# Full attention in a one-core Trainium2 kernel: the turn of a head's result, moved to the shift and undivided

## What is computed

```
h = rmsnorm(X, norm1_w)
q = (h @ wq).reshape(B, S, N_HEADS, D_HEAD)      # k, v likewise
scores = jnp.einsum('bshd,bthd->bhst', q, k) * scale
attn = jax.nn.softmax(scores, axis=-1)
ctx = jnp.einsum('bhst,bthd->bshd', attn, v).reshape(B, S, d)
X = X + ctx @ wo
```

## Time and profile before

| | |
|---|---|
| median of 3 runs | 2958.49 us (2955.47 to 2960.29) |
| the profiled execution | 2950.91 us |
| its span, first to last instruction | 2949.1 us |
| busy: TensorE, VectorE, ScalarE, GpSimd | 88%, 74%, 52%, 10% of the span |
| the full attentions' heads | from 1095 to 1784 us and from 2055 to 2744 us |

### The profile page before, as it was taken

How to read it: one execution, slowest core, us unless ns; L and a number is a source line. 1 busy time by engine, 2 the same in 40 slices (tenths; PEclk the granted TensorE clock), 3 DMA queues, 4 the chain that set the end, 5 groups by cost and what they waited for, 6 DMA issues and landing times. The chain is left out here.

```text
span 2949.1 us, 48804 instructions
## 1 busy us (share of the span) xinstructions
PE 2586.2 (88%) x18006; PEld 1283.9 (44%) x18006; DVE 2196.8 (74%) x5368; ACT 1521.9 (52%) x1907; POOL 291.6 (10%) x598
## 2 busy tenths in 40 slices
PE   6699848789994869999999997995999999999799
PEld 3588725478882531222222215882122222221588
DVE  7644569444445859999999965556999999996554
ACT  2222225432222533777777784222377777778422
POOL 5100021110000110000000001012000000000100
PEclk8799959889996977999999998996799999999899
DMA  2000052000005212111101100001211110110000
GB/s 56 23 16 22 8 124 52 2 23 16 22 8 129 48 42 78 23 23 23 23 15 20 23 2 17 22 11 38 83 23 23 23 23 12 23 23 2 17 22 25
DMA packets 57917, 88.95 MB, mean 30 GB/s; under 512 B 14362, under 2 KB 41184, under 8 KB 57712
## 3 DMA queue, kind: packets, MB, share of 16 engines
q1 hardware_dynamic: 56176, 85.61, 12.4%
q0 software_dynamic: 1536, 0.63, 0.1%
HBM read 57.93 MB, written 26.22 MB: 29 GB/s over the span
## 5 line engine op out<-in xcount | busy, mean ns | idle before, releaser
L1147 DVE TENSOR_REDUCE pair_mx<-ps 128x1 f32<-128x512 f32 x2048 | 1271.1, 685 | 20.1 <-PE ps L990 15.9
L1119 ACT ACTIVATE prob<-ps 128x1024 f32<-128x1024 f32 x1024 | 990.1, 1021 | 249.0 <-PE ps L1025 247.3
L990 PE MATMUL ps<-k_stack,q_stack 48*128 48x512 bf16 x2048 | 642.8, 404 | 55.1 <-PEq L804 12.8
L1039 PE MATMUL ps<-prob,v_head 128*32 128x512 f32 x4096 | 547.2, 606 | 1.3 <-ACT prob L1119 1.0
L990 PEld LDWEIGHTS ps<-k_stack,q_stack 48*128 48x128 bf16 x2048 | 148.6, 93 | 902.4 <-DVE pair_mx L1147 842.7
L1837 DVE TENSOR_TENSOR hid<-silu,ps 128x512 f32<-128x512 f32 x360 | 246.1, 686 | 369.2 <-PE ps L1774 250.3
L1806 ACT ACTIVATE silu<-ps 128x512 f32<-128x512 f32 x360 | 214.7, 597 | 574.6 <-PE ps L1774 566.5
L1025 PE MATMUL ps<-q_stack,k_stack 51*128 51x512 bf16 x2048 | 438.1, 382 | 8.5 <-ACT prob L1119 5.3
L1786 PEld LDWEIGHTS ps<-wd,hid 128*128 128x128 f32 (+1 forms) x2880 | 364.3, 191 | 27.3 <-issue 2.6
L1786 PE MATMUL ps<-wd,hid 128*128 128x128 f32 (+1 forms) x2880 | 368.8, 275 | 0.4
L1774 PE MATMUL ps<-ht_part,wg_part 128*128 128x512 f32 (+1 forms) x1080 | 335.6, 419 | 16.8 <-PEq L311 14.8
(11 more groups left out here) (186 smaller groups left out, 1699.5 us busy)
## 6 DMA issues: line engine op xcount, KB each, us to landing
k_stack<-image_dram SPq DMA_DIRECT2D x96, 192.0 KB, 4.5
q_stack<-image_dram SPq DMA_DIRECT2D x88, 192.0 KB, 4.5
image_dram<-parts SPq DMA_DIRECT2D x4, 1440.0 KB, 12.1
image_dram<-parts SPq DMA_DIRECT2D x4, 1344.0 KB, 9.9
image_dram<-parts SPq DMA_DIRECT2D x4, 960.0 KB, 13.8
image_dram<-parts SPq DMA_DIRECT2D x4, 896.0 KB, 10.9
wg<-in_L_ffn_Wg_dram SPq DMA_DIRECT2D x18, 176.0 KB, 2.3
wu<-in_L_ffn_Wu_dram SPq DMA_DIRECT2D x18, 176.0 KB, 2.4
```

The costliest lines, as they stand in the source:

```text
L990: nc.tensor.matmul(max_bank(n), rows_of(c.q_stack, b, g, ROWS, slice(t * P, (t + 1) * P)), rows_of(c.k_stack, b, g, ROWS, slice(k * CHUNK, ...
L1039: ins = nc.tensor.matmul(out, c.v_head[:, e % 2, kb, :], unit, start=(kb == 0), stop=(kb == TILES - 1), skip_group_check=True)
L1119: nc.scalar.activation(c.prob[:, u % P_UNITS, :], c.ps[:, 2 * (u % 2) * CHUNK:2 * (u % 2) * CHUNK + UNIT], ACT.Exp, scale=scale).then_inc( ...
L1147: nc.vector.reduce_max(mx[:, w:w + 1], max_bank(n), AX.X).then_inc(max_taken.sem, 1)
```

## The change

The turn of head e-1's result now stands in TensorE's order right behind the shift's matmul, ahead of unit 28 of head e (the last head's, as before, at the end of the stage). It goes to bank 3, which is free there as bank 2 is for the shift, and the ring of maxima holds score tiles alone. ScalarE copies the turned result with its sums, undivided, to a new buffer `turned` of 16 x 16 x 9 values a partition, behind its copy of the shift's rows and ahead of exponential 28. Unit 29, whose scores go to banks 2 and 3, waits for that copy too. VectorE's reciprocal and product leave the heads' stage. `output_stage`, for a full attention, begins with four pieces on VectorE, each a reciprocal of 64 sums and a product of 512 values a partition, into `mixed`, which now lies in the second half of `qk`; each piece's transposes wait for it. The windowed attentions are as before.

```diff
@@ full_heads_stage
-    TURN_AT = 24
+    SHIFT_BANK, TURN_BANK = 2, 3
-    place = {}  ... (turns and tiles share the ring's places)
+    place = {(h, w): h * SCORES + w for h in range(HEADS) for w in range(SCORES)}
     def turn(pe, e):
-        n = place["turn", e]
-        pe.wait_ge(*max_taken.after(n - len(MAX_BANKS) + 1))
         pe.wait_ge(*out_taken.after(e + 1))
         for j in range(TPC):
-            ins = nc.tensor.transpose(max_bank(n)[:, j * P:(j + 1) * P], c.out_head[:, e % 2, j * P:(j + 1) * P], c.ident[:])
-        ins.then_inc(max_ready.sem, 1)
+            ins = nc.tensor.transpose(bank(c, TURN_BANK)[:, j * P:(j + 1) * P], c.out_head[:, e % 2, j * P:(j + 1) * P], c.ident[:])
+        ins.then_inc(turned.sem, 1)
     def exp_unit(pe, e, u):
         if u == SHIFT_UNIT and e < HEADS - 1:
             shift_rows(pe, e + 1)
+        if u == SHIFT_UNIT and e:
+            pe.wait_ge(*exp_done.after(unit))
+            turn(pe, e - 1)
         if u == SHIFT_UNIT + 1 and e < HEADS - 1:
             pe.wait_ge(*rows_taken.after(e + 2))
+        if u == SHIFT_UNIT + 1 and e:
+            pe.wait_ge(*turned_taken.after(e))
@@ ScalarE
+            def take_turned(e):
+                act.wait_ge(*turned.after(e + 1))
+                cols = bank(c, TURN_BANK).rearrange("p (j k r) -> p j k r", j=TPC, k=CHUNKS)
+                out = c.turned[:, :, e, :].rearrange("p (k j) r -> p j k r", k=CHUNKS)
+                nc.scalar.activation(out, cols[:, :, :, 0:HD + 1], ACT.Copy).then_inc(turned_taken.sem, 1)
                     if u == SHIFT_UNIT and e < HEADS - 1:
                         take_rows(e + 1)
+                    if u == SHIFT_UNIT and e:
+                        take_turned(e - 1)
             take_out(HEADS - 1)
+            take_turned(HEADS - 1)
@@ VectorE
-            def take_turned(dve, e):
...
-                nc.vector.reciprocal(c.inverse[:], cols[:, :, :, HD]).then_inc(inverted.sem, 1)
...
-                nc.vector.tensor_tensor(out, cols[:, :, :, 0:HD], inverse, ALU.mult).then_inc(max_taken.sem, 1)
@@ output_stage(c, w, dst, divide=False)
             for k in range(CHUNKS):
+                if divide:
+                    pe.wait_ge(*divided.after(k + 1))
                 for t in range(k * TPC, (k + 1) * TPC):
...
+            def divide_piece(k):
+                tiles = slice(k * TPC, (k + 1) * TPC)
+                inverse = c.inverse[:, tiles, :]
+                nc.vector.reciprocal(inverse, c.turned[:, tiles, :, HD]).then_inc(inverted.sem, 1)
+                dve.wait_ge(*inverted.after(k + 1))
+                nc.vector.tensor_tensor(c.mixed[:, tiles, :].rearrange("p t (h d) -> p t h d", d=HD), c.turned[:, tiles, :, 0:HD],
+                                        inverse.rearrange("p t (h o) -> p t h o", o=1).broadcast_to((P, TPC, HEADS, HD)), ALU.mult)\
+                    .then_inc(divided.sem, 1)
+            if divide:
+                for k in range(CHUNKS):
+                    divide_piece(k)
```

More of the change, by code:

```diff
@@ L933, in full_heads_stage @@
     out_taken = c.count("full_out_taken")
-    inverted = c.count("full_sums_inverted")
+    turned = c.count("full_out_turned")
+    turned_taken = c.count("full_turned_taken")
     scale = float(HD) ** -0.5
@@ L1006, in shift_rows @@
             pe.wait_ge(*exp_done.after((e - 1) * EXP_UNITS + SHIFT_UNIT))
-        nc.tensor.matmul(bank(c, 2)[0:PARTS * TILES, 0:P], shift, c.ident16[:], start=True, stop=True).then_inc(rows_ready.sem, 1)
+        nc.tensor.matmul(bank(c, SHIFT_BANK)[0:PARTS * TILES, 0:P], shift, c.ident16[:], start=True, stop=True).then_inc(rows_ready.sem, 1)
     def exp_unit(pe, e, u):
@@ L1071, in _ @@
                 for w in range(SCORES):
-                    if h >= 2 and w == TURN_AT:
-                        turn(pe, h - 2)
                     max_unit(pe, h, w)
@@ L1096, in take_out @@
                 if e >= 2:
-                    act.wait_ge(*max_ready.after(place["turn", e - 2] + 1))
+                    act.wait_ge(*turned.after(e - 1))
                 nc.scalar.activation(c.out_head[:, e % 2, :], bank(c, PV_BANK), ACT.Copy).then_inc(out_taken.sem, 1)
@@ L1105, in take_rows @@
                         act.wait_ge(*shift_loaded[g].after(e * 16))
-                nc.scalar.activation(c.shift_rows[:], bank(c, 2)[0:PARTS * TILES, 0:P], ACT.Copy).then_inc(rows_taken.sem, 1)
+                nc.scalar.activation(c.shift_rows[:], bank(c, SHIFT_BANK)[0:PARTS * TILES, 0:P], ACT.Copy).then_inc(rows_taken.sem, 1)
+            def take_turned(e):
[3 more added lines that the diff above has]
+                nc.scalar.activation(out, cols[:, :, :, 0:HD + 1], ACT.Copy).then_inc(turned_taken.sem, 1)
             take_rows(0)
@@ L1121, in _ @@
             take_out(HEADS - 1)
+            take_turned(HEADS - 1)
         @block.vector
         def _(dve):
-            def take_turned(dve, e):
[L1127 to L1131, removed]
-                nc.vector.reciprocal(c.inverse[:], cols[:, :, :, HD]).then_inc(inverted.sem, 1)
-                dve.wait_ge(*inverted.after(e + 1))
-                out = c.mixed[:, :, e * HD:(e + 1) * HD].rearrange("p (k j) d -> p j k d", k=CHUNKS)
-                inverse = c.inverse[:].rearrange("p j (k o) -> p j k o", o=1).broadcast_to((P, TPC, CHUNKS, HD))
-                nc.vector.tensor_tensor(out, cols[:, :, :, 0:HD], inverse, ALU.mult).then_inc(max_taken.sem, 1)
             for h in range(HEADS):
@@ L1151, in _ @@
                 nc.vector.tensor_reduce(c.rowmax[:], mx.rearrange("p (t k) -> p t k", k=CHUNKS), AX.X, ALU.max, negate=True).then_inc(rowmax_ready.sem, 1)
-            for e in range(HEADS):
-                if turn_at(e)[0] >= HEADS:
-                    take_turned(dve, e)
         @block.gpsimd
@@ L1569, in window_heads_stage, with output_stage @@
         sig.passed(n)
-def output_stage(c, w, dst):
+def output_stage(c, w, dst, divide=False):
     nc = c.nc
@@ L1578, in output_stage @@
     added = c.count("out_added")
+    inverted = c.count("out_sums_inverted")
+    divided = c.count("out_divided")
     with nc.Block() as block:
@@ L1611, in output_stage @@
     added.passed(CHUNKS)
+    if divide:
+        inverted.passed(CHUNKS)
+        divided.passed(CHUNKS)
 def feed_forward_stage(c, dst):
@@ L2101, in attention @@
                     full_heads_stage(c)
-                output_stage(c, w, dst)
+                output_stage(c, w, dst, divide=not paired)
         def experts1():
```

20 lines of the change are left out of this document (9 added, 11 removed).

## The result

The changed kernel takes 2968.06 us at the median of 13 runs (2964.19 to 2971.76), the kernel before, beside it, 2959.77. The ratio is 1.0031 with a 95% interval of 1.0022 to 1.0041, so the change makes the kernel slower by 0.3%, 9 us.

What follows compares the result with a forecast made beforehand. It took a loop through VectorE and TensorE, 2.49 us per four maxima, as the bound. Terms -2.4 + 2.2 + 4.7 + 1.6 = +6.1 us on 2958.5 gave 2964.6 us, range 2959.5 to 2971.

Steps and rivals of the forecast that it cites:

- Rival (c): At the shift: following cycles win the delay back, so the moved turn costs nothing; 2950 us, chance 0.06.
- rival (d): In the ring of maxima: its 0.60 us has another cause and stays; 2981 us, chance 0.04.
- Part 1: Turn leaves the ring of maxima near score 24: 28 x 0.597 = 16.7 us gained.
- Part 2: Turn at unit 28, behind the shift's matmul: 26 x 0.55 = 14.3 us cost (12.5 to 17.2).
- the loops: Turns while maxima run: gain in the ring and cost at the shift together, -2.4 us.
- Rival (b): At the shift, unit 31 becomes the next bound and TensorE waits there too: 8 us more, 2972 us, chance 0.13.
- Part 3: Tails after the last maximum, where ScalarE bounds: +1.1 us a layer, 2.2 in all (1.6 to 3.0).
- Part 4: Output stage: four pieces on VectorE delay the output product by 2.37 us a layer, +4.7 in all (4.0 to 6.0).
- Part 5: Output stage: TensorE's gaps lower its clock, costing 0 to 1.7 us a layer; 0.8 taken, +1.6 in all.
- the windowed row: Trace of a windowed attention's end: after TensorE pauses the granted clock is 0.50 for 3.4 us.
- Rival (a): In the output stage the clock holds; 2963.0 us, chance 0.27.
- the three signs: Wrong if unit 28 no longer delays its pair, four pieces take other than 3.8 us, or the clock stays low long.

Runs made afterwards that it cites:

- the kernel with the filler: The changed kernel with transposes of a constant keeping TensorE busy in the output stage's gaps; ratio 1.0038 to the kernel before.
- second comparison: The changed kernel run again without an edit beside the kernel before; median 2966.54 us, ratio 1.0035.

## Why the prediction was right, and where it was off

**What bounds the kernel.** Right. Away from a turn the pairs are 2.49 us apart in the kernels before and after, and a turn's delay is not won back. The kernel without the turns of heads 0 to 12 shows it from the other side. The prediction's figure for VectorE's own pace, 0.62 us a maximum with a wait in it, is no less than a quarter of 2.49 and shows no slack; the single records do: without a wait the maxima start 0.60 apart, so four take 2.40. Rival (c), a delay regained, and rival (d), a ring that loses its 0.60 for another cause, have both fallen.

**Part 1, the gain.** 0.597 a head was predicted; the period of head 2, which has no turn in the changed kernel, is 39.95 against 40.55 before, 0.60.

**Part 2, the shift.** The mechanism was right, its size low: 0.64 us a head from pair to pair (3.13 - 2.49) instead of 0.55, within the bounds of 0.48 and 0.66. Most of the error is one number. The prediction let the first transpose's weights load 0.10 us behind the shift's; it came after 0.16 (1224.15 to 1224.31). The rest are 0.015 us on ScalarE's copy (0.30 for 0.285) and 0.07 instead of 0.05 from its end to unit 29. Over 26 heads that is 2.3 us, and the loops come out at -0.4 us for both layers instead of -2.4. Rival (b) didn't come: no further wait showed up at unit 31, and the pairs around it (1226.95 and 1229.43) are 2.48 apart.

**Part 3, the tails.** +1.1 us a layer, measured 1.12 and 1.11. At head 15 ScalarE stands still for 1.08 us, where 1.05 to 1.10 was worked out.

**Part 4, the output stage.** The term that was mis-sized. The prediction counts 2.37 us a layer to the first weight load of the output product. It is 3.57: 8.73 us from the last exponential's end (1787.26 to 1795.99), where it was 5.16 (1780.42 to 1785.58). The table above counts to the first matmul, which follows its load by 0.11 us at full clock and 0.22 at half, hence 3.68 there. The step that failed is the reciprocal of 64: it was scaled from 16 elements with the slope of VectorE's products, 1.02 ns an element. The way from the last copy's end to VectorE's first piece was 0.31 us (1790.09 to 1790.40), where 0.29 had been taken; in the kernel that divides in the tail, where no new stage begins in between, it is 0.04 (1793.03 to 1793.07).

**Part 5, the clock.** Right in kind and low in size. 0.8 us a layer was taken of a possible 1.7, from a spell as long as the 3.4 us of the windowed row. The spell was longer: the granted clock is 0.50 from 1792.70 to 1799.40, 6.7 us. Against the kernel with the filler it cost 1.97 and 1.72 us, 0.3 of it ahead of the product's first weight load and the rest behind it. Rival (a), a clock that holds, didn't come in either profile of the unedited changed kernel.

**The sum.** By the stages -0.4 + 2.2 + 7.4 + 2.9 = +12.1 us. With what the low clock costs taken out of the output stage that is -0.4 for the loops, +2.2 for the tails, +6.5 for the pieces and +3.7 for the clock, where -2.4, +2.2, +4.7 and +1.6 were predicted: three of four terms too low by about 2 us each. By the medians it is +8.3 and +11.0 us, by the two ratios +9 and +10. The direction followed from the parts. That the time fell into the range is in part luck: the errors all went the same way, the stages say twice what was forecast, and the range reached to 2971 for the sake of rival (b), which didn't come. Two of the three signs that the prediction named for being wrong did come: the four pieces took 4.84 us and not 3.8, and the clock stayed low through most of the output product. From the last transposes of the heads to the first weight load of the product it took 6.89 us (1789.10 to 1795.99), where 5.6 was forecast.

That the stages say 2 to 3 us more than the ratios stays open. It can be noise: the ratios' intervals are 6.5 to 12.1 and 6.5 to 14.2 us. A clock that held in the executions that weren't profiled is unlikely: the mean granted clock of the changed kernel's six runs in its second comparison is 0.9217, that of the 23 of the kernel before 0.9235. Where it fell in them isn't on record.

## What to carry to other kernels

Work moved off a busy engine is worth nothing by itself. Ask which loop through several engines sets the cycle, and whether the step leaves that loop: here four transposes held TensorE for as long in their new place, and cost, with the copy that follows them, 0.63 us a head beside the shift and 0.42 at unit 20, where they had cost 0.60 in the ring; in the tail a turn costs 0.40. What helps is to make them fewer, as the packing of three heads does. Work that is deferred should go where its engine is idle (the tail), and not to the head of a stage in which the other engines wait for it.

## What the runs showed of the hardware

A VectorE reciprocal costs 6.2 ns an element (0.25 us for 16, 0.55 for 64), six times the 1.02 ns of a product. A product of 512 values read with a stride of nine words takes 0.69 us, as a dense operation of 512 values does. ScalarE's copy of 144 columns, written in runs of nine, takes 0.30 us.

The granted clock fell to 0.50, so 1.2 GHz, in the output stage of every full attention in which the four pieces stood ahead of the transposes without a filler: ten of ten, in the two profiles of the changed kernel and those without the loop's turns, with the turn at unit 20 and with the smaller reciprocals. With the old output stage it held at 1.00 in seven of eight (two profiles of the kernel before, the division in the tail, the three packed heads), and fell once, in the first layer of the packed heads. In that case, as in the seven, TensorE had mostly waited for some 3.5 us behind the last exponential. So the waits at the pieces make the fall likely; they aren't its only cause, and what decides between the one case and the seven isn't shown. It held in two of two where TensorE was kept busy with transposes that nobody reads.
